# A graph attention layer on one core: queries gathered in the same product as values and keys, and copied by ScalarE

## The chip, the cores and the metric

The kernel runs on one core of a Trainium2 chip. The metric is the device time of one execution in microseconds (us), the median of the runs shown. PE is TensorE (PEld its weight loads), DVE is VectorE, ACT is ScalarE, POOL is GpSimd and SP is SyncE.

## The reference, cut to what matters

There are N = 6250 nodes with 256 features and E = 200000 edges (src, dst), sorted by dst. Each node has one of 19 types, and a type has its own weights. Cut to what the change touches:

```python
row, col = (edge_index[0], edge_index[1])          # src, dst
K = typed_linear(x, Wk, bk, node_type)             # 192 wide; Q and V alike
e0, e1, e2 = time_emb of the three times           # cos(log(t + 1) * w + b), 32 wide
def edge_msgs(Kn, Qn, Vn, ek, eq):
    k = jnp.concatenate([Kn, ek], axis=1).reshape(-1, H, DK)     # H = 4, DK = 56
    q = jnp.concatenate([Qn, eq], axis=1).reshape(-1, H, DK)
    att = jnp.einsum('ehd,ed->eh', k, q.sum(axis=1)) / SQRT_DK
    v = jnp.concatenate([Vn, ek], axis=1).reshape(-1, H, DK)
    return (att, v)
att, v = edge_msgs(K[row], Q[col], V[row], e1, e2)
att_i, v_i = edge_msgs(K[col], Q[row], V[col], e2, e1)
att = seg_softmax(att, col, n)
att_i = seg_softmax(att_i, row, n)
agg = segment_sum(v * att, col) + segment_sum(v_i * att_i, row)  # then typed_linear, norms
```

For a score only the sum of a query over the 4 heads is needed, 56 values (DK) a node. Both directions of an edge get a score.

## The kernel before, in words

The kernel is a row of stages, each a block of five engine programs: constants, grouping of the nodes by type, projection (a table in HBM with 440 columns of values, head-summed query and keys for every node), sorting of the edges by owner tile, the score stage (`exchange`), two softmaxes, two weighted sums, and the output. Only the score stage is touched by the change.

In the score stage the edges stand in NT = 1664 tiles of 128, eight tiles (G) a step, 208 steps (NS). An edge has an own node, whose row lies in one known tile of 128 nodes (`tiles[t]`), and another node anywhere. For the own node the stage holds the whole table in SBUF (`tab`, 49 tiles of 440 columns: 192 values, 192 keys, 56 query columns from VK = 384 on) and gathers with a one-hot product: `ohT` (one-hot, transposed) is the stationary operand and 384 columns of `tab` move. For the other node POOL gathers rows from HBM with indirect DMAs (`row`, ring of R = 3). Each step in turn does:

- PE: the angle products of the next step (L1085, two of 384 columns, from `logT` and `blk`), its eight gathers of 384 columns (L1099, three PSUM banks `pG` in turn, from the fourth on each waits for the evacuation of a bank), the transposes for the step after that (L1077, L1079), and the eight query products of 56 columns into `pQ[0]` (L1107), which wait for `s_att`. In fp32 each product is two matmuls and two weight loads in the trace.
- ScalarE: the whole turns (L1013, angle plus a large number, into `turns`), three small copies (L1005 to L1007), the evacuation of each gathered tile in two copies of 192 (values to `pb` L1020, keys to `kc` L1021), the tile-local indices and the gather indices of later steps (L993, L998), the copies of the transposed one-hots and records (L1027, L1029), and five sines (L1035 to L1040).
- VectorE: the one-hots (L1138), the fractions of the turns (L1144), copies and sums of the queries (L1162 to L1165), and four long passes: product and reduction for the other node's keys (L1166, L1167, which signals `s_att`), then for the own node's keys (L1168, L1169, which signals `s_sco`).
- POOL: in step n the eight gathers for step n + 2 (L966, after the scores of step n - 1 and the indices), then, when L1169 of step n is done, three forwards of 128 rows (L1180).
- SP: the stores of values, of scores and of the other five tiles, and the load of records.

Each engine runs its program in order; nothing passes a waiting instruction. Ahead of the steps SP loads `tab` in three pieces of columns (L932 and L935: values, keys, queries), and PE waits for all of them (`NTAB`). The order on ScalarE and on PE is written out in `step` (the functions are printed below). The loop body holds 12 steps.

Of the kernel before, what the change touches and what calls it, by code (L numbers as in the profile page):

```python
# [12 lines left out]
ALU = mybir.AluOpType  # L13
# [848 lines left out]
def exchange(nc, k, S, w_time, b_time, table, recs, spill, mid, runs, bys):  # L862
# [18 lines left out]
    with ExitStack() as ctx:  # L881
# [6 lines left out]
        kc = [s.sb(f"kc{n}", [P, G, KE]) for n in range(2)]  # L888
# [7 lines left out]
        logT = s.sb("logT", [G * REC, P])  # L896
        turns = s.sb("turns", [P, 2, HG, F3])
# [14 lines left out]
        NTAB = 16 * 3 * (1 + (NO > 1))  # L912
# [10 lines left out]
        def _(sp):  # L923
# [6 lines left out]
            for a, b, c in ((0, PROJ, 0), (S.KW + DK, S.TW, PROJ), (S.KW, S.KW + DK, VK)):  # L930
                if NO > 1:
                    sp.dma_start(tab[:, 0:NO - 1, c:c + b - a],  # L932
                                 table[0:(NO - 1) * P, a:b].rearrange("(o p) f -> p o f", p=P)).then_inc(s_tab, 16)
                sp.wait_ge(s_clr, 1)
                sp.dma_start(tab[0:S.LAST, NO - 1, c:c + b - a], table[(NO - 1) * P:N, a:b]).then_inc(s_tab, 16)  # L935
# [52 lines left out]
        def _(act):  # L988
# [20 lines left out]
            def whole_turns(n):  # L1009
                for u in range(2):  # L1010
                    act.wait_ge(s_u[u], n + 1)
                    act.wait_ge(s_fr[u], n)
                    nc.scalar.activation(turns[:, u], pU[u], ACT.Copy, bias=MAGIC).then_inc(s_tu[u], 1)  # L1013

            def gathered(n, j):
                h, q = ring(j, 2), ring(j, R)
                act.wait_ge(s_sco, n - 1 if not isinstance(n, int) else max(n - 1, 0))
                for t in range(G):
                    act.wait_ge(s_gat, n * G + t + 1)
                    nc.scalar.activation(pb[q][:, t, 0:PROJ], pG[t % 3][:, 0:PROJ], ACT.Copy)  # L1020
                    nc.scalar.activation(kc[h][:, t, 0:PROJ], pG[t % 3][:, PROJ:VK], ACT.Copy).then_inc(s_ev, 1)  # L1021

            def transposed(n, j):
                act.wait_ge(s_ot, n + 1)
                if not (isinstance(n, int) and n < 2):
                    act.wait_ge(s_q, n - 1)
                nc.scalar.activation(ohT[ring(j, 2)][:], pO[:], ACT.Copy).then_inc(s_otc, 1)  # L1027
                act.wait_ge(s_lt, n + 1)
                nc.scalar.activation(logT[:], pX[0:G * REC, XT:XT + P], ACT.Copy).then_inc(s_ltc, 1)  # L1029

            def cosines(n, i, j):
# [4 lines left out]
                nc.scalar.activation(kc[h][:, :, PROJ:KE], frac[:, :, 0:TD], ACT.Sin, scale=-2 * math.pi)  # L1036
# [5 lines left out]
            def step(n, i, j, left):  # L1042
# [9 lines left out]
                if left >= 1:  # L1052
                    cosines(n + 1, i, j + 1)

# [10 lines left out]
            cosines(0, 0, 0)  # L1065
            rounds(act, step)

        @block.tensor
        def _(pe):
# [11 lines left out]
            def angles(n):  # L1081
                pe.wait_ge(s_ltc, n + 1)
                for u in range(2):
                    pe.wait_ge(s_fr[u], n)
                    nc.tensor.matmul(pU[u].rearrange("p t f -> p (t f)"), logT[:], blk[:, u * XT:(u + 1) * XT],  # L1085
                                     start=True, stop=True).then_inc(s_u[u], 1)

            def gathers(n, j):
# [5 lines left out]
                for t in range(G):  # L1094
# [16 lines left out]
            def step(n, i, j, left):  # L1111
                if left >= 1:
                    angles(n + 1)
                    tiles = gathers(n + 1, j + 1)
                if left >= 2:
                    transposes(n + 2, i, j + 2)
                if left >= 1:
                    queries(n + 1, j + 1, tiles)
# [4 lines left out]
            tiles = gathers(0, 0)  # L1123
            transposes(1, 0, 1)
            queries(0, 0, tiles)
# [3 lines left out]
        def _(dve):  # L1129
# [10 lines left out]
            def parts_of_turns(n):  # L1140
                dve.wait_ge(s_sinv, n)
                for u in range(2):
                    dve.wait_ge(s_tu[u], n + 1)
                    nc.vector.scalar_tensor_tensor(out=frac[:, u * HG:(u + 1) * HG, :], in0=turns[:, u], scalar=MAGIC, in1=pU[u],  # L1144
                                                   op0=ALU.subtract, op1=ALU.subtract).then_inc(s_fr[u], 1)

            def step(n, i, j, left):
# [10 lines left out]
                ck = c[:].rearrange("p t (h f) -> p t h f", h=H)  # L1158
# [6 lines left out]
                link(nc.vector.tensor_tensor(pQ[0][:, :, QT:DK], pQ[0][:, :, QT:DK], c[:, :, PROJ:KE], ALU.add))  # L1165
# [748 lines left out]
```

## Time and profile before

| what | value |
|---|---|
| time, median of 3 runs | 11668.53 us (11659.7 to 11677.7) |
| span of the profiled execution | 11947.6 us |
| PE, PEld busy | 6482.0, 4341.0 us |
| VectorE, ScalarE, POOL busy | 6497.2, 4337.1, 5738.1 us |
| steady part of the score stage | 3897.4 to 8206.7 us |

The profile is of one execution. A row of a timeline gives the start in us from the span's start, the duration in us, the engine, the line, the operation and the tiles it writes and reads; "x16" means that 16 were merged, and in brackets stands the idle time of the engine before it and what the view holds for its end. Ends of matmuls are modelled. When a semaphore was used before by another stage, the view may name a DMA of that stage.

### The profile page before, as it was taken

The numbers are of one execution on the slowest core, as the hardware profiler recorded it, in microseconds if no ns is written. First come the engines' busy times: TensorE is split into PE (matmuls) and PEld (weight loads), VectorE is DVE, ScalarE is ACT, GpSimd is POOL, SyncE is SP. The second block draws the span as 40 slices with busy tenths as digits, with TensorE's granted clock in tenths as the row PEclk, the third lists the DMA queues.
The fourth block names the chain that finished last, engine by engine and source line by source line (L and its number), as shares of the span: only waits on it lengthen the run. The fifth ranks groups of instructions, "written<-read, shape, count | busy, mean of one in ns | idle before, by whom it ended". The sixth has DMA issues, their size and how long they took to land. (4 is left out here: it accounts for less than half of the span.)

```text
span 11947.6 us, 137428 instructions
## 1 busy us (share of the span) xinstructions
PE 6482.0 (54%) x33872; PEld 4341.0 (36%) x33873; DVE 6497.2 (54%) x13966; ACT 4337.1 (36%) x13263; POOL 5738.1 (48%) x5544
## 2 busy tenths in 40 slices
PE   4865555555553555555555655553111138849966
PEld 2753333333332333333333333331111126637754
DVE  2876666666664455455444554445100028878865
ACT  0012222222221443444343443432100028849963
POOL 6225555555554455555555555555677750003324
PEclk7555555555555677777777777776555559979986
DMA  4120000000001666666666666666666679748872
GB/s 140 42 92 2 2 2 2 2 2 2 2 2 49 193 196 200 197 195 200 195 197 194 203 201 193 197 198 188 220 216 214 208 181 250 236 150 274 280 248 61
DMA packets 1381649, 1740.15 MB, mean 146 GB/s; under 512 B 417563, under 2 KB 1184521, under 8 KB 1381097
## 3 DMA queue, kind: packets, MB, share of 16 engines
q1 hardware_dynamic: 880026, 827.37, 22.6%
q0 software_dynamic: 255392, 657.59, 18.7%
q10 hardware_dynamic: 246064, 253.61, 7.1%
q14 instruction: 140, 1.15, 0.0%
q8 instruction: 27, 0.44, 0.0%
HBM read 1092.74 MB, written 683.17 MB: 149 GB/s over the span
## 5 line engine op out<-in xcount | busy, mean ns | idle before, releaser
L813 POOL DMA_INDIRECT recs<-place_rec,place_addr x1568 | 1586.7, 1012 | 1809.9 <-DVE place_rec L800 1315.1
L1527 PE MATMUL sum_pS<-sum_row,sum_oh 128*128 128x260 f32 x6656 | 1705.1, 411 | 1228.0 <-issue 909.5
L1099 PE MATMUL exch_pG<-exch_tab,exch_ohT 128*128 x3328 | 1540.1, 622 | 1395.6 <-ACT exch_kc L1021 1139.8
L966 POOL DMA_INDIRECT exch_row<-table,exch_of x1664 | 1686.7, 1014 | 556.0 <-issue 505.9
L1527 PEld LDWEIGHTS sum_pS<-sum_row,sum_oh 128*128 128x128 f32 x6656 | 1287.9, 200 | 1644.8 <-issue 1018.1
L1099 PEld LDWEIGHTS exch_pG<-exch_tab,exch_ohT 128*128 128x128 f32 x3328 | 774.2, 243 | 2176.4 <-issue 1957.5
L1180 POOL DMA_INDIRECT bys<-exch_pb x624 | 627.2, 1005 | 1536.2 <-DVE exch_pb L1169 1374.6
L1180 POOL DMA_INDIRECT bys<-sum_pb x960 | 1015.3, 1058 | 355.9 <-issue 309.5
L1144 DVE SCALAR_TENSOR_TENSOR exch_frac<-exch_turns,exch_pX 128x384 f32<-128x384 f32 x208 | 115.2, 554 | 1812.7 <-ACT exch_turns L1013 1266.8
L1575 DVE TENSOR_TENSOR edge_acc<-edge_acc,sum_pS 128x260 f32 x832 | 352.3, 423 | 1330.1 <-DMA soft_key<-keys 925.5
L1543 ACT ACTIVATE sum_off<-kept_ramp,sum_neg 128x128 f32<-128x128 f32 x3328 | 1014.5, 387 | 0.0
L1490 POOL TENSOR_TENSOR sum_row<-sum_row,agg_al 128x448 f32<-128x448 f32 x208 | 277.0, 1332 | 1478.6 <-DMA sum_row<-bys 1478.6
L1549 ACT ACTIVATE sum_oh<-sum_off 128x1024 f32<-128x1024 f32 x416 | 439.8, 1057 | 1391.0 <-DMA soft_key<-keys 935.9
L776 DVE SCALAR_TENSOR_TENSOR place_junk<-place_pB,place_own_g,sort_tri 128x128 bf16<-128x128 f32 x3136 | 880.3, 347 | 19.2 <-issue 16.1
L704 PE MATMUL place_pB<-place_rows,sort_sel 64*128 64x512 bf16 x784 | 463.6, 592 | 563.5 <-DVE place_junk L776 395.3
L1020 ACT ACTIVATE exch_pb<-exch_pG 128x192 f32<-128x192 f32 x1664 | 555.7, 334 | 500.3 <-PE exch_pG L1099 335.5
L655 ACT ACTIVATE place_t_lo<-place_pT 128x1024 f16<-128x1024 bf16 x392 | 398.5, 1017 | 851.3 <-remote 648.6
L1013 ACT ACTIVATE exch_turns<-exch_pX 128x384 f32<-128x384 f32 x208 | 101.3, 487 | 1522.0 <-DMA joint<-in_x 1376.0
L697 PE MATMUL place_pT<-kept_ident_b,sort_oh_lo 128*128 128x128 bf16 x3136 | 432.6, 313 | 352.1 <-ACT place_t_lo L655 280.1
L719 PE MATMUL place_pC<-sort_oh_hi,sort_oh_lo 128*128 128x49 bf16 x3136 | 422.6, 274 | 268.0 <-issue 264.0
L714 PE MATMUL place_pL<-place_cur,place_t_lo 128*128 128x49 f16 x6272 | 405.4, 219 | 295.7 <-issue 289.0
L659 ACT ACTIVATE place_whole<-place_pC 128x392 f32<-128x392 f32 x394 | 194.2, 493 | 992.3 <-remote 969.2
(280 smaller groups left out, 12837.9 us busy)
## 6 DMA issues: line engine op xcount, KB each, us to landing
spill<-exch_row SPq DMA_DIRECT2D x208, 1024.0 KB
sum_row<-bys SPq DMA_DIRECT2D x208, 1024.0 KB
sum_row<-spill ACTq DMA_DIRECT2D x206, 1024.0 KB
mid<-exch_pb SPq DMA_DIRECT2D x208, 660.0 KB
sum_pb<-mid SPq DMA_DIRECT2D x192, 660.0 KB
exch_row<-table,exch_of POOLq DMA_INDIRECT x1664
recs<-place_rec,place_addr POOLq DMA_INDIRECT x1568
bys<-sum_pb POOLq DMA_INDIRECT x960
```

Source lines behind the costliest of these rows:

```text
L697: last = nc.tensor.transpose(pT[:, t, :], oh_lo[:, par, u % 2, :, u // 2 * LN + t], k.ident_b[:])
L704: nc.tensor.matmul(pB[b][:], sel[:, u % 2 * 4 + u // 2 * 2 + b, :], rows[:, par], start=True, stop=True).then_inc(s_b[b], 1)
L719: last = nc.tensor.matmul(pC[d][:, t * NO:(t + 1) * NO], oh_lo[:, par, d, :, c], oh_hi[:, par, d, :, c], start=False, stop=True, skip_grou ...
L776: last = nc.vector.scalar_tensor_tensor(out=junk[:, b, t, :], in0=pB[b][:, t, :], scalar=own_g[:, par, d, c:c + 1], in1=tri[:], op0=ALU.is ...
L813: nc.gpsimd.indirect_dma_start(recs, bass.IndirectOffsetOnAxis(addr[:, par, 0, t:t + 1], 0), rec[:, par, t, :], None, bounds_check=last_sl ...
L966: nc.gpsimd.indirect_dma_start(row[q][:, t, TD:TD + S.TW], None, table, bass.IndirectOffsetOnAxis(of[q][:, t:t + 1], 0), bounds_check=last ...
L1020: nc.scalar.activation(pb[q][:, t, 0:PROJ], pG[t % 3][:, 0:PROJ], ACT.Copy)
L1099: nc.tensor.matmul(pG[t % 3][:, 0:VK], ohT[ring(j, 2)][:, t, :], flat[:, bass.ds(tiles[t] * GW, VK)], start=True, stop=True).then_inc(s_ga ...
L1180: return nc.gpsimd.indirect_dma_start(bys, bass.IndirectOffsetOnAxis(pb[:, t, S.SLOTC:S.SLOTC + 1].bitcast(I32), 0), pb[:, t, :], None, bo ...
L1527: last = nc.tensor.matmul(pS[j % SETS * HG + t // 2][:, 0:AW], oh[h][:, t, :], row[j][:, t, :], start=(t % 2 == 0), stop=(t % 2 == 1))
L1543: last = nc.scalar.activation(off[:, t, :], k.ramp[:], ACT.Abs, bias=neg[h][:, t:t + 1])
L1549: nc.scalar.activation(oh[h][:], off[:], ACT.Relu, bias=1.0, scale=-1.0).then_inc(s_oh, 1)
```

## The change

Queries are no longer gathered by products of their own. The gather product of a tile is 440 columns wide (GW) and leaves values, queries and keys in one PSUM bank; the table's columns in SBUF stand in that order, so that two pieces are loaded and not three. ScalarE's second copy takes the queries along with the keys (`kc` is DK = 56 columns wider), and a new ScalarE instruction, `queries`, copies the eight tiles' queries from `kc` to `pQ[0]` in PSUM after the sines of the step; it waits for `s_att` as PE's `queries` did, which is gone. To make room in SBUF the whole turns go to `frac` and the fractions are made there in place (so ScalarE waits for `s_sinv` ahead of them), and `logT` lies in the constant `below`. ScalarE's copy of ohT waits for the gathers (`s_gat`) instead of the queries (`s_q`).

```diff
-        kc = [s.sb(f"kc{n}", [P, G, KE]) for n in range(2)]
+        kc = [s.sb(f"kc{n}", [P, G, DK + KE]) for n in range(2)]
...
-        logT = s.sb("logT", [G * REC, P])
-        turns = s.sb("turns", [P, 2, HG, F3])
+        logT = k.below[0:G * REC, :]
...
-        NTAB = 16 * 3 * (1 + (NO > 1))
+        NTAB = 16 * 2 * (1 + (NO > 1))
...
-            for a, b, c in ((0, PROJ, 0), (S.KW + DK, S.TW, PROJ), (S.KW, S.KW + DK, VK)):
+            for a, b, c in ((0, PROJ, 0), (S.KW, S.TW, PROJ)):
...
             def whole_turns(n):
+                act.wait_ge(s_sinv, n)
                 for u in range(2):
                     act.wait_ge(s_u[u], n + 1)
                     act.wait_ge(s_fr[u], n)
-                    nc.scalar.activation(turns[:, u], pU[u], ACT.Copy, bias=MAGIC).then_inc(s_tu[u], 1)
+                    nc.scalar.activation(frac[:, u * HG:(u + 1) * HG, :], pU[u], ACT.Copy, bias=MAGIC).then_inc(s_tu[u], 1)
...
-                    nc.scalar.activation(kc[h][:, t, 0:PROJ], pG[t % 3][:, PROJ:VK], ACT.Copy).then_inc(s_ev, 1)
+                    nc.scalar.activation(kc[h][:, t, 0:DK + PROJ], pG[t % 3][:, PROJ:GW], ACT.Copy).then_inc(s_ev, 1)
+
+            def queries(n, j):
+                act.wait_ge(s_ev, (n + 1) * G)
+                act.wait_ge(s_att, n)
+                nc.scalar.activation(pQ[0][:], kc[ring(j, 2)][:, :, 0:DK], ACT.Copy).then_inc(s_q, 1)
...
                 if not (isinstance(n, int) and n < 2):
-                    act.wait_ge(s_q, n - 1)
+                    act.wait_ge(s_gat, (n - 1) * G)
...
                 if left >= 1:
                     cosines(n + 1, i, j + 1)
+                    queries(n + 1, j + 1)
...
-                    nc.tensor.matmul(pG[t % 3][:, 0:VK], ohT[ring(j, 2)][:, t, :], flat[:, bass.ds(tiles[t] * GW, VK)],
+                    nc.tensor.matmul(pG[t % 3][:, 0:GW], ohT[ring(j, 2)][:, t, :], flat[:, bass.ds(tiles[t] * GW, GW)],
                                      start=True, stop=True).then_inc(s_gat, 1)
-                return tiles
-
-            def queries(n, j, tiles):
-                flat = tab[:].rearrange("p o f -> p (o f)")
-                pe.wait_ge(s_att, n)
-                for t in range(G):
-                    last = nc.tensor.matmul(pQ[0][:, t, :], ohT[ring(j, 2)][:, t, :], flat[:, bass.ds(tiles[t] * GW + VK, DK)],
-                                            start=True, stop=True)
-                last.then_inc(s_q, 1)
...
                 for u in range(2):
                     dve.wait_ge(s_tu[u], n + 1)
-                    nc.vector.scalar_tensor_tensor(out=frac[:, u * HG:(u + 1) * HG, :], in0=turns[:, u], scalar=MAGIC, in1=pU[u],
+                    part = frac[:, u * HG:(u + 1) * HG, :]
+                    nc.vector.scalar_tensor_tensor(out=part, in0=part, scalar=MAGIC, in1=pU[u],
                                                    op0=ALU.subtract, op1=ALU.subtract).then_inc(s_fr[u], 1)
```

## Rows read from the trace of the kernel before

**Rows 1.** Page, head: span; busy us, share of the span, instructions.

```profile
span 11947.6 us, 137428 instructions
...
PE 6482.0 (54%) x33872; PEld 4341.0 (36%) x33873; DVE 6497.2 (54%) x13966; ACT 4337.1 (36%) x13263; POOL 5738.1 (48%) x5544
```

**Rows 2.** Busy time by stretch (bounds, length, engines), granted clock, DMA share, GB/s.

```profile
3897.40:8206.70 4309.30, 2449.44 (x9351) 1479.40 (x9351) 2200.90 (x2078) 1773.98 (x6233) 2286.76 (x2261) 0.72 0.64 196
```

**Rows 3.** Waits of the score stage: total us, times, longest.

```profile
ACT exch_turns L1013 <- DMA joint<-in_x: 1376.0, 95, 21.4
POOL bys L1180 <- DVE exch_pb L1169: 1374.6, 108, 49.5
```

**Rows 4.** Timeline of POOL, one pair of steps.

```profile
6003.00 1.02 POOL L1180 DMA_INDIRECT bys<-exch_pb  x1 [14.64 <-DVE exch_pb L1169]
...
6030.71 1.00 POOL L966 DMA_INDIRECT exch_row<-table,exch_of  x1 [0.30 <-issue]
6042.61 1.02 POOL L1180 DMA_INDIRECT bys<-exch_pb  x1 [10.91 <-DVE exch_pb L1169]
```

**Rows 5.** Timeline of PE, the same pair.

```profile
6001.93 0.81 PE L1085 MATMUL exch_pU<-exch_blk,exch_logT 64*128 64x384 f32 x2
6002.66 5.43 PE L1099 MATMUL exch_pG<-exch_tab,exch_ohT 128*128 x16
...
6009.22 1.99 PE L1107 MATMUL exch_pQ<-exch_tab,exch_ohT 128*128 x16 [0.52 <-issue]
```

**Rows 6.** Timeline of ScalarE, the same pair.

```profile
6002.80 0.48 ACT L1013 ACTIVATE exch_turns<-exch_pU 128x384 f32<-128x384 f32 x1
...
6010.29 1.03 ACT L1027 ACTIVATE exch_ohT<-exch_pO 128x1024 f32<-128x1024 bf16 x1 [1.40 <-remote]
6011.69 0.27 ACT L1029 ACTIVATE exch_logT<-exch_pX 64x128 f32<-64x128 f32 x1 [0.37 <-remote]
...
6028.84 0.49 ACT L1013 ACTIVATE exch_turns<-exch_pX 128x384 f32<-128x384 f32 x1 [15.13 <-DMA joint<-in_x]
6031.66 0.49 ACT L1013 ACTIVATE exch_turns<-exch_pU 128x384 f32<-128x384 f32 x1 [2.33 <-DMA proj_xr<-in_x,kept_nodes]
```

**Rows 7.** Timeline of VectorE, the same pair.

```profile
6033.71 2.02 DVE L1166 TENSOR_TENSOR exch_row<-exch_row,exch_pQ 128x1792 f32<-128x1792 f32 x1
...
6039.74 2.02 DVE L1169 TENSOR_REDUCE exch_pb<-exch_kc 128x32 f32<-128x1792 f32 x1
```

**Rows 8.** Timeline of ScalarE, evacuations of two consecutive tiles elsewhere.

```profile
6678.47 0.33 ACT L1020 ACTIVATE exch_pb<-exch_pG 128x192 f32<-128x192 f32 x1 [2.35 <-PE exch_pG L1099]
...
6681.37 0.33 ACT L1020 ACTIVATE exch_pb<-exch_pG 128x192 f32<-128x192 f32 x1 [2.34 <-PE exch_pG L1099]
```

**Rows 9.** Timeline of SP, loads of the table's second and third pieces.

```profile
3859.53 3.77 SPq L932 DMA_DIRECT2D exch_tab<-table  x1
...
3884.87 1.90 SPq L932 DMA_DIRECT2D exch_tab<-table  x1
```

**Rows 10.** Groups of the page by line: busy us, mean ns, idle before.

```profile
L1020 ACT ACTIVATE exch_pb<-exch_pG 128x192 f32<-128x192 f32 x1664 | 555.7, 334 | 500.3 <-PE exch_pG L1099 335.5
...
L1013 ACT ACTIVATE exch_turns<-exch_pX 128x384 f32<-128x384 f32 x208 | 101.3, 487 | 1522.0 <-DMA joint<-in_x 1376.0
```

**Rows 11.** Timeline of POOL, two restarts, the longest rhythm.

```profile
5452.14 1.02 POOL L1180 DMA_INDIRECT bys<-exch_pb  x1 [14.54 <-DVE exch_pb L1169]
...
5495.23 1.02 POOL L1180 DMA_INDIRECT bys<-exch_pb  x1 [14.54 <-DVE exch_pb L1169]
```

**Rows 12.** Timeline of POOL, first and last of five restarts.

```profile
6629.71 1.02 POOL L1180 DMA_INDIRECT bys<-exch_pb  x1 [8.88 <-DVE exch_pb L1169]
...
6700.91 1.02 POOL L1180 DMA_INDIRECT bys<-exch_pb  x1 [2.93 <-DVE exch_pb L1169]
```

**Rows 13.** Timeline of ScalarE, two turns released together.

```profile
7146.52 0.49 ACT L1013 ACTIVATE exch_turns<-exch_pX 128x384 f32<-128x384 f32 x1 [18.08 <-DMA joint<-in_x]
7146.91 0.48 ACT L1013 ACTIVATE exch_turns<-exch_pU 128x384 f32<-128x384 f32 x1
```

More of the change, by code:

```diff
@@ L1025, in transposed @@
                 if not (isinstance(n, int) and n < 2):
-                    act.wait_ge(s_q, n - 1)
+                    act.wait_ge(s_gat, (n - 1) * G)
                 nc.scalar.activation(ohT[ring(j, 2)][:], pO[:], ACT.Copy).then_inc(s_otc, 1)
                 act.wait_ge(s_lt, n + 1)
-                nc.scalar.activation(logT[:], pX[0:G * REC, XT:XT + P], ACT.Copy).then_inc(s_ltc, 1)
+                nc.scalar.activation(logT, pX[0:G * REC, XT:XT + P], ACT.Copy).then_inc(s_ltc, 1)
             def cosines(n, i, j):
@@ L1035, in cosines @@
                 nc.scalar.activation(pb[q][:, :, PROJ:PROJ + 2 * TD], frac[:, :, 0:2 * TD], ACT.Sin, scale=-2 * math.pi)
-                nc.scalar.activation(kc[h][:, :, PROJ:KE], frac[:, :, 0:TD], ACT.Sin, scale=-2 * math.pi)
+                nc.scalar.activation(kc[h][:, :, DK + PROJ:DK + KE], frac[:, :, 0:TD], ACT.Sin, scale=-2 * math.pi)
                 act.wait_ge(s_row[q], 16 * G * (turn_of(i, j, R, PER) + 1))
@@ L1065, in _ @@
             cosines(0, 0, 0)
+            queries(0, 0)
             rounds(act, step)
@@ L1084, in angles @@
                     pe.wait_ge(s_fr[u], n)
-                    nc.tensor.matmul(pU[u].rearrange("p t f -> p (t f)"), logT[:], blk[:, u * XT:(u + 1) * XT],
+                    nc.tensor.matmul(pU[u].rearrange("p t f -> p (t f)"), logT, blk[:, u * XT:(u + 1) * XT],
                                      start=True, stop=True).then_inc(s_u[u], 1)
@@ L1113, in step @@
                     angles(n + 1)
-                    tiles = gathers(n + 1, j + 1)
+                    gathers(n + 1, j + 1)
                 if left >= 2:
                     transposes(n + 2, i, j + 2)
-                if left >= 1:
-                    queries(n + 1, j + 1, tiles)
             transposes(0, 0, 0)
@@ L1122, in _ @@
             angles(0)
-            tiles = gathers(0, 0)
+            gathers(0, 0)
             transposes(1, 0, 1)
-            queries(0, 0, tiles)
             rounds(pe, step)
@@ L1157, in step @@
                 rk = row[q][:, :, RQ + DK:RW].rearrange("p t (h f) -> p t h f", h=H)
-                ck = c[:].rearrange("p t (h f) -> p t h f", h=H)
+                ck = c[:, :, DK:DK + KE].rearrange("p t (h f) -> p t h f", h=H)
                 dve.wait_ge(s_sin, n + 1)
@@ L1164, in step @@
                 dve.wait_ge(s_q, n + 1)
-                link(nc.vector.tensor_tensor(pQ[0][:, :, QT:DK], pQ[0][:, :, QT:DK], c[:, :, PROJ:KE], ALU.add))
+                link(nc.vector.tensor_tensor(pQ[0][:, :, QT:DK], pQ[0][:, :, QT:DK], c[:, :, DK + PROJ:DK + KE], ALU.add))
                 link(nc.vector.tensor_tensor(rk, rk, bc(pQ[0][:], 2, H), ALU.mult))
```

## The prediction

> **What bounds the kernel now.** I read the page's first line for the size of each engine's work [rows 1], then the stage's stretch of the span [rows 2]. The reader is to see that the score stage takes 4309.3 us of steady work, and that no engine is full in it: POOL, the busiest, works 2286.76 of the 4309.3 us. The steady part has 208 steps of 8 tiles (the count of the 128x384 turns), so 4309.3/208 = 20.72 us a step. Nothing outside this stage is touched, except that the constant `below` is overwritten after its last use.
>
> Next the waits of the stage [rows 3]. POOL waits for the scores in L1169 1374.6 us in 108 waits, one wait for about two steps. ScalarE waits 1376.0 us ahead of L1013 for an event that the view calls a DMA; L1013 waits only for PE's angle products (L1085) and for VectorE, so the name is wrong, and I go by times. VectorE waits for ScalarE's L1013. The loop is therefore PE, ScalarE, VectorE, POOL.
>
> Then one pair of steps in order of time. POOL issues without a gap from 6003.00: three forwards, eight row gathers, three forwards, eight gathers, to 6031.71, and then waits 10.91 us [rows 4]. That pace, 28.7 us for two steps or 14.4 a step, is the floor. PE's own records of that pair end early: the queries (L1107) at 6011.21 [rows 5], and the angles that follow wait only for L1029, which ends at 6011.96 [rows 6]. But ScalarE, idle, takes the first angles at 6028.84 and the second at 6031.66 [rows 6], 17 and 20 us after that; in the calm stretch the same hand-over took no time (the second angles end at 6002.74, the second turns start at 6002.80) [rows 5, 6]. VectorE's products of the step, whose other inputs were ready, begin at 6033.71 and end at 6041.76 [rows 7], and POOL restarts at 6042.61 [rows 4]. So PE's results reach the others late for as long as POOL's row gathers run, and the lateness counts in PE instructions: one weight load and one matmul (L1079) separate the starts of L1027 at 6010.29 and L1029 at 6011.69, 1.40 us; two of each separate the two turns, 2.82 us [rows 6]; in another stretch the evacuations of consecutive tiles, again two and two, are 2.90 us apart [rows 8]. That is 0.70 us an instruction, against 5.43 us for 16 matmuls and their loads when nothing interferes [rows 5]. Between the release of L1029 (6011.69) and the first turns (6028.84) lie 17.15 us, and in PE's queue there stand the 32 instructions of the queries and 4 of the first angles. What slows PE's completions the trace doesn't tell; I read only that it is counted by the instruction.
>
> **The change part by part.**
> Table load. The third of three pieces is issued at 3884.87 and the steady part begins at 3897.4, 12.5 us; the second takes 25.3 [rows 2, 9]. Its columns join the keys' piece, which then is 248 wide instead of 192: 25.3 x 248/192 = 32.7 against 37.8, so 5 us less; between 0 and 12.5. I take 5.
>
> PE, removed: 8 query products, 16 matmuls and 16 loads a step. Undisturbed they cost 1.99 us [rows 5] and hide beside ScalarE's copies of ohT and logT (1.03 + 0.27 us [rows 6]) whole: they are through at 6011.21, and the angles wait for 6011.96 anyway [rows 5, 6]. Under POOL's gathers they cost up to 32 x 0.70 = 22.6 us, and the 36 instructions with the angles took 17.15 us in the pair shown. They stand ahead of the next angles, which gate turns, fractions and, in VectorE's order, the products of the step before.
>
> PE, added: 56 columns in 16 matmuls. 5.43 us x 56/384 = 0.79 us a step at 2.4 GHz, up to twice that at 1.2 GHz (the mean granted clock is 0.72 of full [rows 2]). No instruction is added, so the 0.70 us each would not grow.
>
> ScalarE, added: the key copy is 248 instead of 192 wide. From 0.334 us at 192 [rows 10] to 1.03 at 1024 elements (L1027 [rows 6]) a column costs 0.83 ns: 56 x 8 x 0.83 = 0.37 us a step. One copy of the queries to PSUM, 8 x 56 = 448 elements, takes about the 0.487 us of the turns of 384 [rows 10] and 64 elements more, 0.54. Together 0.91 us on a queue that is 41% busy (1773.98 of 4309.3 us [rows 2]); it lies on the path only when ScalarE runs late.
>
> Waits. ScalarE's queries wait for `s_att` of the step before (L1167). Behind them are queued the next turns, the owners and the evacuations, and PE (its 3 banks), VectorE (fractions) and POOL (indices) wait for those. L1167 is over when two passes of 2.02 us (L1168, L1169) are still to come, 4 us before VectorE is free for the next fractions [rows 7]; the copy of the queries and the turns take ScalarE about 1 us of these 4. So VectorE isn't held up, 0; what can come later is the evacuations, by 0 to 2 us when VectorE is late. VectorE's wait for the queries moves from PE to ScalarE, whose copy ends 0.5 us after its last sine; L1162 and L1163 come first on VectorE (they lie in the 2.05 us between the second turns at 6031.66 and L1166 at 6033.71 [rows 6, 7]) and cover it, 0 to 0.5 us. The wait for `s_sinv` ahead of the turns is for ScalarE's own instruction before it, 0 to 0.2 us. The turns now go to `frac` in place, same shapes, 0; the buffer that is dropped and the wait for `s_gat` in place of `s_q` cost 0, because the gathers of two steps back have long ended.
>
> The sum for the pair shown. Without the queries the first angles need 4 x 0.70 = 2.8 us from 6012.0, the second 2.8 more: 6017.6 instead of 6031.66. From there the old intervals hold: fraction and products begin 2.0 us later, the scores 8.05 us after that, 6027.7. That is before POOL's last gather of the pair ends (6031.71), so POOL's wait of 10.91 us for the scores goes. What is late next: POOL's indices (L998), which ScalarE writes after the eight evacuations. At 2.90 us each from 6017.6 five or six tiles are through when the gathers' traffic has ended (I take 3 us after POOL's last issue, 6034.7) and the others take about 2: the next gather starts near 6036.7 instead of 6046.7. The stage should thus leave the two-step rhythm (43.1 us between restarts of POOL in its longest form [rows 11], 41.4 in the mean) for the one-step rhythm that the trace already has in one place: five restarts from 6629.71 to 6700.91, 71.2 us for four steps, 17.8 each [rows 12]. I add 0.8 us for the wider products, which are on the path there; ScalarE's part lies in its waits. That is 18.6 us, and I leave a fifth of the steps as they are now: 0.8 x 18.6 + 0.2 x 20.7 = 19.0. (20.72 - 19.0) x 208 = 358 us, plus 5. The profiled execution is 11947.6 us [rows 1], 279.1 over the median of 11668.53; I carry the difference over: 11947.6 - 363 = 11585, and 11668.5 - 363 = **11305 us**. Own range of this case: 17.8 to 20.3 us a step, that is 11060 to 11580.
>
> **The rivals.**
> No change: what delays PE's signals is the traffic as such, and they come free only when it ends, queries or not. For it: at 7146.52 and 7146.91 both turns are released 0.39 us apart after an idle time of 18.08 us [rows 13], a burst and not 0.70 us an instruction. Then POOL's 28.7 us, the tail of the traffic and 11 us to the scores make the same rhythm; 11668.5 - 5 = 11663, from 11640 to 11700. The same time results if the delay belongs to the profiled execution alone. The Trainium skill (SBUF — State Buffer, section "Who interferes with whom") states that DMA never contends with a compute engine and that PE waits on nobody. By it the removed queries are worth only their hidden 1.99 us, which is this rival; the trace, with signals 16 us late beside gathers, speaks against the rule.
>
> Slower: PE reaches the transposes of ohT (L1077) late. They are just ahead of the slow stretch now (L1027 starts at 6010.29, after 1.40 us of idle time [rows 6]). The wider products move them back by 0.8 us, in the half-clock tiles by more, and ScalarE's 0.9 us moves the turns of the pair's second step. Then the eight transposes themselves fall under the gathers, and every pair takes the longest rhythm, 43.1 us [rows 11], or 21.55 a step: + 0.83 x 208 = 173 us, about 11840, from 11720 to 11900. It decides if the angles don't get out before the gathers' end, that is if more than about 15 us pass from L1029's release to the second turns although only 8 instructions stand between.
>
> More: POOL never waits, 14.4 us a step; 6.3 x 208 = 1310 us, 10350. Against it: the one-step stretch, where POOL still waits 2.93 us a step [rows 12]. Anything below 11060 goes here.
>
> The change doesn't do what it says (the wait on `s_att` puts ScalarE's turns behind VectorE, and it hands back what PE saves): between the first two rivals in time, and counted there.
>
> **How the numbers follow.** Forecast case 0.56 (11305); more than forecast 0.07; no change 0.14, of which 0.02 falls below and 0.01 above the 0.2% (23 us, about what a measurement of this kernel can tell from no change); slower 0.23. So faster 0.65, same 0.11, slower 0.24. The range goes from 11060 to 11790: it leaves out the 0.07 below and about 0.12 of the slower case above.
>
> **What the profile after would show.** Right: ScalarE's wait ahead of the turns falls from 1376 to under 700 us; POOL's wait for L1169 comes nearly once a step and is short; no wait over 10 us; the turns follow logT's release by 6 to 8 us under gathers. POOL's issues stay at 1.0 us, products of 440 columns take 56/384 more, ScalarE's busy time rises by 0.91 x 208 = 189 us. Wrong: pairs of 43 us with a POOL wait of 14.5 us remain (no change), or nearly all pairs have it and L1027 is released late (slower).

## The result and the profile after

The changed kernel takes 11296.69 us (median of 4 runs, 11283.37 to 11331.65) against 11672.14 us (4 runs, 11659.7 to 11677.7): a ratio of 0.9689, with a 95% interval of 0.9672 to 0.9706, so it is 375 us faster. The forecast was 11305.

The head of the page of the changed kernel (span; busy us, share of the span, instructions), to be read beside [rows 1]:

```profile
span 11281.3 us, 129743 instructions
...
PE 6436.5 (57%) x30544; PEld 3960.9 (35%) x30545; DVE 6503.4 (58%) x13966; ACT 4500.4 (40%) x13471; POOL 5722.0 (51%) x5544
```

VectorE and POOL do the same work as before, ScalarE 163.3 us more, PE a little less in 3328 fewer matmuls (16 x 208). Busy time has not been saved; waiting has. The score stage from its first angle to its last score, columns as in [rows 2]:

```profile
3860.20:7556.30 3696.10, 2421.28 (x6023) 1109.81 (x6023) 2211.09 (x2078) 1939.99 (x6441) 2288.56 (x2261) 0.74 0.74 229
```

3696.1 / 208 = 17.77 us a step, against 20.72, both in the one profiled execution of each kernel. From the issue of the table's load to the first angle it is 52.8 us (55.2 before). The waits of this stretch, as [rows 3]: total us, times, longest.

```profile
POOL bys L1176 <- DVE exch_pb L1165: 442.4, 92, 48.1
...
POOL exch_row L965 <- ACT exch_of L997: 250.3, 45, 8.5
...
ACT exch_frac L1013 <- DMA proj_xr<-in_x,kept_nodes: 114.7, 44, 4.4
...
ACT exch_frac L1013 <- issue: 104.6, 54, 50.8
```

POOL's wait for the scores (L1165 now, L1169 before) fell from 1374.6 to 442.4 us. The 1376.0 us that ScalarE waited ahead of the turns under the name of `joint<-in_x` are gone; what is left ahead of L1013 is 114.7 and 104.6 us, 50.8 of these the stage's start, and 21.8 us under PE's own name. New is POOL's wait for the indices (L997), 250.3 us in 45 waits, which the prediction had named as what is late next. Both can be seen in POOL's timeline (start, us, engine and line, idle time before and what ended it), as [rows 4, 11, 12]:

```profile
4566.91 1.02 POOL L1176 DMA_INDIRECT bys<-exch_pb  x1 [12.13 <-DVE exch_pb L1165]
```

```profile
5689.62 1.02 POOL L1176 DMA_INDIRECT bys<-exch_pb  x1 [9.28 <-DVE exch_pb L1165]
...
5720.47 1.02 POOL L1176 DMA_INDIRECT bys<-exch_pb  x1 [1.85 <-issue]
...
5727.34 1.05 POOL L965 DMA_INDIRECT exch_row<-table,exch_of  x1 [3.26 <-ACT exch_of L997]
...
5741.50 1.02 POOL L1176 DMA_INDIRECT bys<-exch_pb  x1 [3.98 <-DVE exch_pb L1165]
```

12.13 us is the longest wait for scores after the stage's start; four are over 10 us, and 14.5 us [rows 11] does not come back in this trace. Between 5689.62 and 5741.50 lie three steps, 51.88 / 3 = 17.3 us each, which contain waits of 1.85, 3.26 and 3.98 us. ScalarE in the same place, where POOL issues row gathers, as [rows 6, 8]:

```profile
5704.06 0.26 ACT L1034 ACTIVATE kept_below<-exch_pX 64x128 f32<-64x128 f32 x1
...
5706.70 0.49 ACT L1013 ACTIVATE exch_frac<-exch_pX 128x384 f32<-128x384 f32 x1 [0.22 <-issue]
5709.52 0.49 ACT L1013 ACTIVATE exch_frac<-exch_pU 128x384 f32<-128x384 f32 x1 [2.33 <-DMA proj_xr<-in_x,kept_nodes]
...
5716.62 0.33 ACT L1020 ACTIVATE exch_pb<-exch_pG 128x192 f32<-128x192 f32 x1 [3.65 <-DMA slots<-group_none]
...
5719.45 0.33 ACT L1020 ACTIVATE exch_pb<-exch_pG 128x192 f32<-128x192 f32 x1 [2.23 <-PE exch_pG L1106]
...
5725.43 0.37 ACT L1021 ACTIVATE exch_kc<-exch_pG 128x248 f32<-128x248 f32 x1
...
5726.26 0.23 ACT L997 ACTIVATE exch_of<-exch_rec 128x8 int32<-128x8 f32 x1
```

The lateness of PE's results has not gone: the two turns are 2.82 us apart, two evacuations 2.83. What has gone is the 32 query instructions that stood in that slow queue. The copy of logT begins at 5704.06 and the second turns at 5709.52, 5.5 us later; in the pair of before 20.0 us lay between them (6011.69 and 6031.66 [rows 6]). The indices (5726.26) come out behind the last evacuation, and POOL goes on at 5727.34, 0.85 us after their end. The pace isn't one figure: of the seven intervals between this step's eight evacuations (from 5712.37) one is 4.25 us, one 2.83, four are 1.42 to 1.45, and the last is 0.48.

The trace also keeps a time for each semaphore event that was recorded, that is, for the moment at which an engine's signal was raised. These times show the lateness directly. (Each event is set against the last instruction with its semaphore that had ended, so lateness isn't overstated.) In the score stage of the kernel before, all 3849 recorded events of ScalarE and VectorE come 0.01 us after the end of their instruction. Of PE's 2415 events 820 come more than 0.5 us after the modelled end of their product, up to 23.65 us. All of these come during an indirect DMA of POOL or at most 3.5 us after one; of the 860 PE events outside these stretches none is late. In the pair of [rows 4, 5] the events of L1079, of the queries and of the two angle products lie at 6011.67, 6026.00, 6028.82 and 6031.64. So the 32 query instructions took 14.33 us there, 0.45 us each, and the four of an angle product 2.82 us, 0.70 each. In the changed kernel 591 of PE's 1840 events are late, up to 9.68 us.

### The profile page after: what moved, and what is told of

The parts are those of the page before. It is cut to its first block and busy times, and to the rows that moved or that the text cites. A ratio compares the mean times of both kernels' runs of the same rounds, so it can differ in the third digit from the quotient of the medians.

```text
span 11281.3 us, 129743 instructions
## 1 busy us (share of the span) xinstructions
PE 6436.5 (57%) x30544; PEld 3960.9 (35%) x30545; DVE 6503.4 (58%) x13966; ACT 4500.4 (40%) x13471; POOL 5722.0 (51%) x5544
## 5 line engine op out<-in xcount | busy, mean ns | idle before, releaser
L813 POOL DMA_INDIRECT recs<-place_rec,place_addr x1568 | 1584.8, 1011 | 1780.8 <-DVE place_rec L800 1286.8
L1106 PE MATMUL exch_pG<-exch_tab,exch_ohT 128*128 x3328 | 1822.0, 701 | 579.6 <-issue 480.8
L1092 PE MATMUL exch_pX<-exch_blk,kept_below 64*128 64x384 f32 x416 | 264.1, 726 | 733.6 <-issue 394.0
L1021 ACT ACTIVATE exch_kc<-exch_pG 128x248 f32<-128x248 f32 x1664 | 624.9, 376 | 0.0
L1133 DVE TENSOR_TENSOR exch_oh<-exch_lob,kept_ramp 128x1024 bf16<-128x1024 bf16 x208 | 143.1, 688 | 744.1 <-PE exch_pO L1084 377.8
```

The costliest lines, as they stand in the source:

```text
L813: nc.gpsimd.indirect_dma_start(recs, bass.IndirectOffsetOnAxis(addr[:, par, 0, t:t + 1], 0), rec[:, par, t, :], None, bounds_check=last_sl ...
L1021: nc.scalar.activation(kc[h][:, t, 0:DK + PROJ], pG[t % 3][:, PROJ:GW], ACT.Copy).then_inc(s_ev, 1)
L1106: nc.tensor.matmul(pG[t % 3][:, 0:GW], ohT[ring(j, 2)][:, t, :], flat[:, bass.ds(tiles[t] * GW, GW)], start=True, stop=True).then_inc(s_ga ...
```

## The experiments

Two theories stood against each other. Mine: while POOL issues its row gathers, PE's completions reach the others late, by the instruction, and the change gains by taking 32 instructions a step out of that queue. The rivals: it is the wide product or the order that counts; it is the data that the gathers move; it is the profiled execution alone. Each run was timed beside the kernel before on the same chip. The first four ran together. Where an experiment has a time for a step, it is the mean distance of POOL's first forwards; measured so, the kernel before has 20.69 us and the changed one 17.72 in the profiles of the result.

### The stage twice, in both kernels

```
+            exchange(nc, k, S, w_time, b_time, table, recs, spill, mid, runs, bys, "again")
+            Scope.retire(nc)
```

> The kernel before with the score stage run twice, one after the other (the second run computes the same again), so that the time less 11672 is the stage's time outside a profile. In its profile the stage takes 4366 us (3840.4 to 8206.7). Theory A (the slow completions of PE are real, but a part of them exists only while a profile is taken, since the span was 275 us over the median before and nothing over it after): +4090 us, 11672 + 4090 = 15760, 19.4 us a step. Rival (the profile tells the stage's time as it is, and what the execution without it saves lies in other stages): +4366, 16040.

> The changed kernel with the score stage run twice. In its profile the stage takes about 3717 us (3840 to 7557). Theory A and the rival agree, as its span and median are alike: +3700, 11297 + 3700 = 15000. The difference to the kernel before with two stages, less the single difference of 375, is the gain of one stage once more: A expects 375, the rival 650.

Measured: 16338.02 us for the kernel before with a second stage (1.3719, interval 1.3654 to 1.3784, before: 11919.42) and 15342.67 for the changed one (1.2878, 1.2817 to 1.2939). The second stage costs 16338 - 11919 = 4419 us in the timed runs, which is what a profile shows of one. So the slow rhythm is in the timed runs in full, 20.6 and 20.7 us a step in the two stages. The expectation of a shorter stage in the timed runs (+4090 us) falls; the one of a second stage as long as the profiled one (+4366) is near. But every timed run here has a span and a granted clock on record, so something was recorded in each of them. The runs show that the lateness is in the times that are compared, and not that it is there without any recording.

The difference of the two is 995 us for two stages, 498 each if both gain alike. The changed kernel alone was not timed on this chip; less the 375 us above, as the expectation had it, the second stage's gain would be 620 us. The profiles show 461 us for the first stage and 507 for the second, and 18.4 and 18.2 us a step in the changed kernel. So on this chip the change is worth more than 375 us.

### The queries left out, and the wide product alone

```
-                if left >= 1:
-                    queries(n + 1, j + 1, tiles)
```

> The kernel before with PE's query products left out and nothing in their place (the scores of one direction are then meaningless). Theory A (32 PE instructions fewer under POOL's gathers are the whole gain; the wider products and ScalarE's copy are a cost): faster than the change, about 17.2 us a step in the profile, 11297 - 0.6 x 208 = 11170, from 11050 to 11250. Rival (what helps is not the removal but something else, such as the wait on the scores of the step before leaving PE, or two table pieces instead of three): the same idea gives 11300 if the wait counts, 11670 if neither.

With the products go PE's wait for `s_att` and VectorE's for `s_q`, and the copy of ohT waits for the gathers, as in the change.

Measured: 11443.84, 0.9604 (0.9559 to 0.965), 476 us less, 18.3 us a step. The waits of its stage:

```profile
POOL bys L1169 <- DVE exch_pb L1158: 715.6, 104, 49.5
...
POOL exch_row L966 <- ACT exch_of L998: 148.8, 26, 8.2
...
ACT exch_turns L1013 <- DMA joint<-in_x: 43.2, 21, 3.0
```

```
-  nc.tensor.matmul(pG[t % 3][:, 0:VK], ..., flat[:, bass.ds(tiles[t] * GW, VK)], ...
+  nc.tensor.matmul(pG[t % 3][:, 0:GW], ..., flat[:, bass.ds(tiles[t] * GW, GW)], ...
```

> The kernel before with gather products of 440 columns instead of 384 and the query products still there: the price of the added columns alone. Theory A: they fall into the calm stretch, + 0.8 us in a loop with slack of several us, between 0 and + 170 us, I expect 11720. Rival (PE's time by columns is the bound): + 0.79 to 1.6 us a step, 11840 to 12000.

Measured: 11929.94, 1.0004 (0.9981 to 1.0027). Its waits are those of before:

```profile
ACT exch_turns L1013 <- DMA joint<-in_x: 1399.0, 98, 22.1
POOL bys L1180 <- DVE exch_pb L1169: 1369.0, 104, 49.5
```

Taking the query products away gives the whole gain, and the wait ahead of the turns goes with them (43.2 us left of about 1400). The 56 columns more cost nothing in the kernel before. The expectation that this run would be faster than the change missed: the change has 18.4 and 18.2 us a step on this chip, this run 18.3, and 498 us a stage stand against 476. So ScalarE's 0.9 us a step cost nothing that these runs can tell either; the interval of the 476 is about 55 us to either side.

### How many instructions, how many columns, how much data

These ran together on another chip, with the change once more.

> The changed kernel as it is, beside the experiments on one chip, since the kernel before took 11919 us on the chip of the last runs and 11672 on the first. Theory A (PE's completions are slowed by the instruction under POOL's gathers, and 32 fewer of them are the gain): as without queries at all, ratio 0.96 to 0.97. Rival (the wide products or ScalarE's work cost what b_noq does not pay): 0.01 above b_noq's 0.960.

Measured: 11312.35 against 11661.28, 0.9698 (0.9676 to 0.9721), 17.80 us a step: the result repeats.

```
-                for t in range(G):
+                for t in range(G // 2):
```

> The kernel before with query products for four of the eight tiles of a step (the other four tiles' queries stay as they are in PSUM, so half the scores of one direction are meaningless). Theory A, by the instruction: 16 fewer, about half the gain, ratio 0.98, from 0.97 to 0.99. Rival (the queries cost as a whole, by their hand-over and wait, whatever their number): as before, 1.00. Another rival (a threshold: the angles get out in time or not): 0.96.

```
-  last = nc.tensor.matmul(pQ[0][:, t, :], ..., flat[:, bass.ds(tiles[t] * GW + VK, DK)],
+  last = nc.tensor.matmul(pQ[0][:, t, 0:8], ..., flat[:, bass.ds(tiles[t] * GW + VK, 8)],
```

> The kernel before with query products of 8 columns instead of 56, their number unchanged (the other 48 columns are not computed). Theory A: the number of instructions counts, not their width: ratio 1.00, 0.995 to 1.005. Rival (PE's reads of moving data are what the gathers' traffic slows): most of the gain, 0.965.

```
-  nc.gpsimd.indirect_dma_start(row[q][:, t, TD:TD + S.TW], None, table,
+  nc.gpsimd.indirect_dma_start(row[q][:, t, TD:TD + REC], None, recs,
```

> The kernel before with POOL's row gathers as many as before but of 32 bytes a row (from another tensor) instead of 1888, so that POOL issues the same and nearly no data moves (the other nodes' queries and keys are then not the table's). Theory A1, the data in flight slow PE: PE is free, POOL's issues are the bound, 14.4 to 15 us a step, ratio 0.89 to 0.91. Rival A2, POOL's making of the descriptors slows PE: the rhythm stays, ratio 0.99 to 1.0.

In the half and the narrow run `pQ[0]` is set to zero once ahead of the steps. In the light run a row has 32 bytes instead of 1888 (the table in HBM has 472 columns; its copy in SBUF has 440), and the row tiles are zeroed first. The packets stay nearly as many, 1328415 against 1381649 in the kernel before.

Measured: half the queries 11454.07, 0.9817 (0.9798 to 0.9837), 18.50 us a step; 8 columns instead of 56 in all of them 11662.19, 0.9992 (0.9968 to 1.0017), 19.75 a step; gathers of 32-byte rows, as many of them, 11580.49, 0.9927 (0.9898 to 0.9955), 19.22 a step. The waits of the three, in this order:

```profile
POOL bys L1181 <- DVE exch_pb L1170: 749.7, 99, 49.7
ACT exch_turns L1013 <- DMA joint<-in_x: 586.0, 81, 11.9
```

```profile
POOL bys L1181 <- DVE exch_pb L1170: 1153.3, 116, 48.5
ACT exch_turns L1013 <- DMA joint<-in_x: 1072.0, 93, 21.1
```

```profile
POOL bys L1183 <- DVE exch_pb L1172: 1000.7, 122, 14.4
ACT exch_turns L1014 <- DMA joint<-in_x: 903.8, 93, 17.9
```

The longest wait ahead of the turns is 11.9 us with 16 query instructions in the queue and 21.1 with 32 narrow ones: (21.1 - 11.9) / 16 = 0.58 us an instruction, between the 0.45 and the 0.70 of the semaphore events. Half the instructions give 207 of the 349 us, and PE's wait for `s_att` is still there, so it isn't the wait that costs. Six sevenths of the columns give nothing: it is the count of instructions. That alone doesn't tell lateness from PE's plain time, for the 16 narrow products take 1.95 us in PE's records and the full ones 1.99. With most of the gathers' data gone, about 115 GB/s instead of about 210 in the stage's slices of the page, the long waits stay and the time falls by 81 us: the bytes are a small part of the cause. PE's events are still up to 22.52 us late, 876 of 2311. What stays is POOL's issuing of 8 gathers a step, and the number of packets.

### The same chip as in the first four, in another condition

The last four ran on the chip of the first four, but there the kernel before now took 8952.69 us (24 runs, 8938.51 to 8967.26) where it had taken 11919.42. Nothing of the kernel had changed. They must be read against that time.

> The kernel before without the query products once more, beside other runs: on another chip it gave 0.960, and the change 0.970 here. Theory A: the added columns (b_wide: nothing) and ScalarE's copies cost little, so 0.965 to 0.975. Rival (ScalarE's 0.91 us a step and its wait hand back a part): 0.955 to 0.962.

```
-                for t in range(G):
+                for t in [*range(G), *range(G)]:
```

> The kernel before with every query product issued twice, 32 more PE instructions a step. Theory A, by the instruction: as much slower as the change is faster, ratio 1.03, from 1.02 to 1.06. Rival (a longest rhythm of 43 us for two steps that more instructions cannot lengthen): 1.00 to 1.01 on a chip that is in it already, 1.02 on the other.

Measured: without the queries, the same kernel as above, 8955.06, 1.0006 (0.9996 to 1.0015); with the queries twice 8964.42, 1.0014 (1.0004 to 1.0024). Leaving the queries out doesn't gain what it gained in the other condition, and doubling them costs next to nothing; doubled queries were not run in the other condition. The same program in both, busy time by thirds of the kernel (placement, score stage, the rest; PE, PEld, DVE, ACT, POOL, clock, DMA share, GB/s). First in the long condition:

```profile
0.00:3835.00 3835.00, 2072.73 (x17043) 1408.88 (x17044) 2484.90 (x9110) 881.62 (x1815) 1854.79 (x1862) 0.52 0.08 23
3835.00:7700.00 3865.00, 2274.37 (x6023) 1159.10 (x6023) 2207.44 (x2075) 1784.99 (x6233) 2313.18 (x2284) 0.69 0.71 223
7700.00:11445.00 3745.00, 1969.75 (x7478) 1451.23 (x7478) 1819.21 (x2783) 1680.06 (x5215) 1562.21 (x1399) 0.72 0.72 211
```

Then in the short one:

```profile
0.00:2894.00 2894.00, 1928.39 (x17034) 1374.15 (x17035) 2462.62 (x9108) 902.11 (x1809) 1879.14 (x1860) 0.53 0.10 30
2894.00:5980.00 3086.00, 2008.42 (x6032) 1067.32 (x6032) 2192.15 (x2079) 1743.13 (x6241) 2310.19 (x2285) 0.83 0.88 280
5980.00:8960.00 2980.00, 1910.27 (x7478) 1455.61 (x7478) 1814.53 (x2781) 1679.32 (x5215) 1495.11 (x1399) 0.82 0.85 265
```

All three thirds are 20 to 25% shorter, with nearly the same busy time on VectorE, ScalarE and POOL (POOL's last third differs most, 1562.21 and 1495.11): the difference is mostly waiting, everywhere. Memory traffic is faster too: the busiest slice of the page has 280 GB/s in the long condition and 393 in the short. Which waiting, the placement stage shows (waits of 1000 to 2800 us, the same program; the short condition gets through more rounds in it, so the longest waits compare and the totals don't), in the long condition

```profile
POOL recs L813 <- DVE place_rec L800: 581.6, 58, 11.2
ACT place_whole L659 <- remote: 564.6, 94, 10.3
```

and in the short one

```profile
POOL recs L813 <- issue: 437.2, 1324, 2.2
...
ACT place_whole L659 <- PE place_pC L719: 109.5, 248, 0.5
```

Here too POOL issues indirect DMAs (L813), and ScalarE waits for PE's product up to 10.3 us in the one (the view has no name for what ends this wait, "remote") and at most 0.5 us in the other, though the DMA queues are only 2 and 3% busy in this stretch. The events of that product (L719) come up to 9.91 us late in the long condition, half of them over 2 us, and 0.01 us after its end in the short one. In the score stage with the queries twice, PE, POOL and ScalarE in order of time in the short condition:

```profile
4532.35 0.91 PE L1085 MATMUL exch_pX<-exch_blk,exch_logT 64*128 64x384 f32 x2
4532.61 1.05 POOL L966 DMA_INDIRECT exch_row<-table,exch_of  x1 [0.30 <-issue]
...
4533.10 0.80 PE L1085 MATMUL exch_pU<-exch_blk,exch_logT 64*128 64x384 f32 x2
4533.29 0.49 ACT L1013 ACTIVATE exch_turns<-exch_pX 128x384 f32<-128x384 f32 x1 [0.74 <-PE exch_pX L1085]
...
4533.94 0.49 ACT L1013 ACTIVATE exch_turns<-exch_pU 128x384 f32<-128x384 f32 x1 [0.15 <-PE exch_pU L1085]
4533.98 1.02 POOL L966 DMA_INDIRECT exch_row<-table,exch_of  x1 [0.32 <-issue]
...
4537.67 0.33 ACT L1020 ACTIVATE exch_pb<-exch_pG 128x192 f32<-128x192 f32 x1 [0.20 <-PE exch_pG L1099]
...
4538.10 1.00 POOL L966 DMA_INDIRECT exch_row<-table,exch_of  x1 [0.30 <-issue]
...
4538.31 0.33 ACT L1020 ACTIVATE exch_pb<-exch_pG 128x192 f32<-128x192 f32 x1
...
4538.96 0.33 ACT L1020 ACTIVATE exch_pb<-exch_pG 128x192 f32<-128x192 f32 x1
```

POOL issues a row gather every 1.31 us, and the turns follow PE's angles at once, 0.65 us apart and not 2.82; the evacuations are 0.64 us apart and not 2.9. In this condition PE's completions are not late: in the two traces none of PE's 5170 events in the stage comes later than 0.01 us. POOL hardly waits at all (14.5 us a step without the queries, 14.6 with them twice). So there should be nothing for the change to gain; the changed kernel itself was not run here, only with a reordering (below).

The two conditions differ in one more thing. In the long one many semaphore events are missing from the trace: 1625 of 7889 of the compute engines' in the score stage of the kernel before, 2898 of 7771 after the change. In the short one there are 50 missing of 7890 with the queries twice, and 10 of 7684 without. The kernel without queries has 50215 events in all in the one and 132045 in the other, with instructions and DMA packets alike. So recording itself may be what is congested in the long condition, and what holds PE up. No run tests this rival.

```
+                sp.dma_start(row[q][:, :, TD:TD + S.TW], table[0:P * G, :].rearrange("(p t) f -> p t f", p=P)).then_inc(s_row[q], 16)
...
-                    nc.gpsimd.indirect_dma_start(row[q][:, t, TD:TD + S.TW], None, table,
```

> The kernel before with the rows of the other nodes loaded by one plain DMA a step from SP's queue (1024 consecutive rows of the table, not those of the edges), the same bytes into the same tiles, and POOL left with the three forwards a step. Theory A2 (b_light: hardly any data moved and the gain was 0.007, so it is POOL's issuing and not the data that slows PE): PE is free, the bound is VectorE's 10.6 us or the transfers' 4 MB, 11 to 13 us a step, ratio 0.84 to 0.88. Rival A1 (DMA traffic of any kind slows PE): above 17 us a step, ratio over 0.96.

Measured: 8470.40, 0.9465 (0.9449 to 0.9481), 12.24 us a step. The stage's busy time and POOL's group on the page:

```profile
2950.00:5500.00 2550.00, 2150.00 (x9302) 1340.79 (x9300) 2189.35 (x2075) 1724.72 (x6207) 616.63 (x624) 0.92 0.97 332
```

```profile
L1176 POOL DMA_INDIRECT bys<-exch_pb x624 | 616.6, 988 | 2024.8 <-DVE exch_pb L1165 1893.1
```

With one plain load a step in place of the eight gathers POOL is 24% busy and waits for the scores in every step; VectorE at 86% and the DMA queues at 0.97 are next. The expected 11 to 13 us a step came; the expected ratio of 0.84 to 0.88 was reckoned from the long condition. So the 14.5 us a step of the short condition are POOL's eleven issues (11 x 1.31 = 14.4), as the prediction's floor had it. Whether a plain load of the same data would also have left PE's completions in peace, which is what this run was for, can't be read from it, since in this condition nothing disturbed them.

```
-                    gathered(n + 1, j + 1)
                 if left >= 3:
                     ...
                     sources(n + 3, i, j + 3)
+                if left >= 1:
+                    gathered(n + 1, j + 1)
```

> The changed kernel with ScalarE writing the tile indices and POOL's gather indices (lows, sources) before the evacuations of the step and not behind them. In the profile after POOL waits 289 us for L997. Theory: that wait goes and a part of it comes back as waits for the scores: 50 to 200 us, ratio to the kernel before 0.955 to 0.965. Rival (POOL then issues more without a gap, and PE is slowed for longer, so that nothing is gained): 0.970.

Measured: 8975.42, 1.0024 (1.0014 to 1.0034), 14.64 us a step. It was to take away the wait for the indices that the change leaves behind, and in this condition that wait hardly exists:

```profile
POOL exch_row L965 <- ACT exch_of L997: 9.4, 1, 9.4
```

This is also the only timing of the changed code in the short condition: no gain over the kernel before. Against the 250.3 us of the long condition the edit could have brought something; that was not tried there and stays open.

## Why the prediction was right, and where it was not

**Mechanism.** PE's results late beside POOL's gathers, counted by the instruction, and the queries' 32 instructions in front of the angles: shown, in the long condition, by four runs. None of the queries: 0.9604. Half of them: 0.9817. All of them narrow: 0.9992. The wide product alone: 1.0004. The times alone would also fit a plainer account, that PE's time for the queries is on the path: 476 / 208 = 2.3 us a step is near their 1.99 us, and half of them gave 1.0. Against it stand the semaphore events, by which the queries of the pair take 14.33 us; the wait ahead of the turns, which falls by more than 1300 us; and the short condition, where twice the queries cost 12 us in all at 14.6 us a step. That the gain of 1.8 us a step is smaller than the lateness taken away is no contradiction: only what POOL waits for the scores can be gained, and behind it come the indices.

The Trainium skill (SBUF — State Buffer, section "Who interferes with whom"), which speaks of the ports to SBUF, states that PE never waits on anyone and that DMA never contends with a compute engine. In the short condition the time goes by it (1.0006). In the long one the time doesn't (0.9604), but no run shows that a port is what PE waits for there.

**PE, added, 0.79 us a step.** As an undisturbed duration right: the 16 wide products take 6.30 us at 5692.49 where 5.43 x 440/384 = 6.22 was to be expected. As a term of the sum too high: I had put it on the path, and 1.0004 (+-0.0023, or 27 us, 0.13 us a step) says that it is not in the kernel before. In the changed one 18.4 and 18.2 us a step against 18.3 without queries say the same.

**ScalarE, added, 0.91 us a step.** Sizes right. The key copies, of which the second line is the run with half the queries:

```profile
L1021 ACT ACTIVATE exch_kc<-exch_pG 128x248 f32<-128x248 f32 x1664 | 624.9, 376 | 0.0
```

```profile
L1021 ACT ACTIVATE exch_kc<-exch_pG 128x192 f32<-128x192 f32 x1664 | 547.9, 329 | 0.0
```

77 us for 208 steps is 0.37 a step, and the copy of the queries takes 0.53. ScalarE's busy time rose by 163.3 us, not 189, since part of these runs into the next instruction. Nothing of it showed on the path.

**Table load.** -2.4 us instead of -5, within 0 to -12.5.

**The pair's chain.** Without the queries the second turns were to follow 5.6 us after logT's release (8 x 0.70); in the pair shown 5.5 us. The 0.70 us an instruction holds for the angles and not for the queries, whose 32 took 0.45 us each by their event; the prediction's 22.6 us for them was too much, and its sum did not use it. The next late thing was to be the indices behind the evacuations: so it is, 250.3 us.

**The stage's step, 19.0 us.** This is the step that failed. It came out at 17.77, just under the stated 17.8 to 20.3. I had left a fifth of the steps as they were and added 0.8 us for the wider products; neither is in the trace. I had also named the one-step rhythm as what comes, with POOL's wait nearly once a step and none over 10 us. POOL waits for the scores 92 times in 208 steps, as seldom as before (108), and four times over 10 us after the start (24 and 20 times in the two stages of the doubled run); the rhythm of two and three steps stays, and only what it loses per round is smaller. So the place of the gain was right and its form wrong.

**Carrying the difference over.** The time came out right because a second error stood against the first. I took 20.72 us a step from an execution of 11947.6 us and subtracted the gain from runs of 11668.5. The spans of the two profiles differ by 666.3 us: (20.72 - 17.77) x 208 = 614 in the stage, 2.4 in the load, the other 50 in code that the change does not touch. The runs differ by 375. In the runs of the study the profiled execution is one of the timed ones and within 40 us of their median, and 11947.6 lies where the chip of the first four experiments had its kernel before (11871.91 to 11974.37). So that execution most likely stood under other circumstances than the runs of 11668.5; no run settles which. With nearly their time, 11662.19, the kernel with narrow queries has 19.75 us a step. From there to 17.80 the gain is 1.95 x 208 = 406 us; the two profiled executions differ by 393, the medians of the two kernels by 350. From 20.72 to 19.0 it was 358. Too high a start and too high an end had nearly the same difference, and that was luck.

**The rivals.** No change (0.14) is what the short condition shows, as far as it was run (1.0006 without queries, 1.0024 for the reordered change), and for a reason that I had not given: not that the traffic delays everything alike, but that nothing is late. Slower (0.23): the transposes did fall late in places, L1032 is released after an idle of 3.50 us at 5703.14, but no pair of 43.1 us came of it. More (0.07): 14.5 to 14.6 us a step is what the short condition has, with twice the queries or with none; the change has no part in it.

**What stays open.** What makes PE's completions late. They are late beside POOL's indirect DMAs in two stages, at a DMA share of 0.74 and of 0.02, and hardly less with small rows; so the issuing is suspected and not the bytes, but no run has taken the issuing away in the long condition, none has changed the number of packets alone, and none has been timed without recording, whose events are missing in the long condition. What is counted isn't separated either: a query product left out takes two matmuls, two weight loads and one further instruction with it (8319 fewer on the page in 208 steps). And what puts one chip now into the one condition and now into the other: between the two lay only time.

## What to carry to other kernels

When an engine's results reach the others later than its own records end, count the instructions that stand in its queue ahead of the ones that matter, not their columns: joining small products to a large one that is issued anyway can then pay although they are hidden by PE's own records (here 1.8 us a step, 375 us in all), and half the instructions give a good half of the gain (207 of 349 us). Compare the semaphore events with the ends of the instructions where the trace has them: they tell a late signal from a long instruction. Look first whether the lateness is in the timed runs of the day: repeat the stage or leave the suspected part out, beside the kernel before on the same chip, and take the start of the sum and the time that it is subtracted from from the same execution. A gain that rests on such a lateness is worth nothing where the chip doesn't show it.

## What the runs showed of the hardware

The same kernel took 11919 us and, later, 8953 us on the same chip, with ranges of 1% and 0.3%; without the queries, where both were profiled, VectorE, ScalarE and POOL have nearly equal busy time. In the long condition PE's signals come up to 23.65 us after the modelled end of the product, 0.45 to 0.70 us an instruction in the pair shown, and only during an indirect DMA of POOL or within 3.5 us after it; ScalarE's and VectorE's come 0.01 us after the end in the same stretch. In the short one PE's come 0.01 us after the end too, at the same pace of issue. In both an indirect DMA costs POOL 1.0 us and 0.3 us to the next, and this alone is the floor of the stage, 14.4 us; one plain load in place of eight gathers lowered the step to 12.24 us.
